# The last group's v beside and behind the last q and k, in a decoder layer on one core

## The reference, cut to what matters

```python
# B, S, D = 16, 128, 256; H, DH = 8, 64; f32 throughout
q, k, v = x @ W_q.T, x @ W_k.T, x @ W_v.T            # q, k: 512 wide, v: 256 wide
b = (q * k).reshape(B, S, H, DH).sum(-1) / sqrt(DH)
a = -softplus(x @ W_alpha_w.T + W_alpha_b).reshape(B, S, H, DH).sum(-1)
vs = where(sign(v) == 0, 1, sign(v)); vl = log(abs(v) + 1e-8)
# scan over time per batch and head, in logs: ln = lse(a_t + ln, b_t), nm likewise with b_t + vl_t,
#   y_t = sum over heads of sign * exp(nm - ln)
x = layernorm(x + y @ W_o.T)
x = layernorm(x + cross_attention_of_8_experts(x))    # relu(x @ in_e.T) @ out_e.T, gated
x = layernorm(x + three_layer_ffn(x))
```

## Time and profile before

| | us |
|---|---|
| median of 3 runs (lowest, highest) | 799.23 (799.13, 799.63) |
| the profiled execution's own time | 798.58 |
| its span, first to last instruction | 796.8 |
| mean granted clock, as a share of full speed | 0.998 |
| TensorE busy | 783.4 |
| VectorE, ScalarE, GpSimd busy | 473.9, 355.1, 199.8 |

### The profile page before, as it was taken

The page is one execution under the profiler, slowest core; times in us unless marked ns, Lnnn a source line. Parts: engine busy times, 40 slices in busy tenths (PEclk is TensorE's granted clock), DMA queues, the critical chain, the costliest instruction groups (busy, mean ns, idle before and its releaser), DMA issues.

```text
span 796.8 us, 12545 instructions
## 1 busy us (share of the span) xinstructions
PE 783.4 (98%) x3879; PEld 660.4 (83%) x3879; DVE 473.9 (59%) x1125; ACT 355.1 (45%) x683; POOL 199.8 (25%) x230
## 2 busy tenths in 40 slices
PE   8999989999999999999999999999999999999996
PEld 6888968888888888888888888888888888888885
DVE  4788878876686868778665664126422552255124
ACT  6788633444343434343443364434543354335331
POOL 3776143225352525344342310000000000000000
PEclk9999999999999999999999999999999999999999
DMA  9600000003113121311211000000000000000000
GB/s 335 207 1 0 2 1 1 1 1 107 56 52 107 49 85 53 105 53 55 92 41 53 4 5 1 1 0 27 0 0 0 26 0 0 0 19 9 1 0 30
DMA packets 15748, 31.45 MB, mean 39 GB/s; under 512 B 1616, under 2 KB 6224, under 8 KB 15440
## 3 DMA queue, kind: packets, MB, share of 16 engines
q1 hardware_dynamic: 15264, 30.04, 11.7%
q10 hardware_dynamic: 432, 0.79, 0.3%
HBM read 28.72 MB, written 2.10 MB: 39 GB/s over the span
## 4 chain that ended last, share of the span: by engine, by line
PE 93%; DVE 3%; issue 1%; DMA 1%; ACT 0%; POOL 0%; DVEq 0%; SPq 0%
PE bank L1046 29%; PE bank L961 14%; PE bank L838 9%; PE bank L866 8%; PE bank L939 7%; PE bank L940 7%; PE bank L944 7%; PE bank L960 6%; PE bank L1061 3%; PE bank L964 2%; DMA wp_lo_f<-in_wproj 1%; DVE x_tok L1184 1%; DVE hx_lo L1273 0%; PE bank L924 0%; PE bank L983 0%
## 5 line engine op out<-in xcount | busy, mean ns | idle before, releaser
L961 PE MATMUL bank<-wx_both,hx_hi 128*128 128x512 f32 x512 | 191.4, 397 | 0.0
L721 ACT ACTIVATE hx_hi<-bank 128x512 fp32r<-128x512 f32 x128 | 76.5, 598 | 205.3 <-PE bank L944 205.3
L537 POOL TENSOR_TENSOR x_tok<-right,x_tok 128x256 f32<-128x256 f32 x128 | 98.2, 768 | 212.2 <-ACT right L728 212.2
L1273 DVE SCALAR_TENSOR_TENSOR hx_lo<-bank,hx_hi 128x512 fp32r<-128x512 f32 x128 | 87.9, 687 | 66.6 <-ACT hx_hi L721 66.3
L961 PEld LDWEIGHTS bank<-wx_both,hx_hi 128*128 128x128 f32 x512 | 96.0, 188 | 16.7
L960 PE MATMUL bank<-wx_both,hx_lo 128*128 128x256 f32 x384 | 108.6, 283 | 0.0
L939 PE MATMUL bank<-xT_hi,wx_both 128*128 128x512 f32 x256 | 100.5, 392 | 0.9 <-ACT xT_hi L714 0.5
L1046 PE MATMUL bank<-ha_hi_r,wf_hi_r 128*128 128x512 f32 x256 | 100.0, 391 | 0.0
L1046 PE MATMUL bank<-hb_hi_r,wf_hi_r 128*128 128x512 f32 x256 | 99.9, 390 | 0.0
L940 PE MATMUL bank<-xT_hi,wx_both 128*128 128x512 f32 x256 | 99.7, 389 | 0.0
L1046 PE MATMUL bank<-ha_lo,wf_hi_r 128*128 128x512 f32 x256 | 99.6, 389 | 0.0
(11 more groups left out here) (157 smaller groups left out, 1443.2 us busy)
## 6 DMA issues: line engine op xcount, KB each, us to landing
stage<-in_wffn SPq DMA_DIRECT2D x44, 256.0 KB, 2.6
wx_raw<-in_wx SPq DMA_DIRECT2D x16, 512.0 KB, 3.7
x_tok<-in_x SPq DMA_DIRECT2D x1, 2048.0 KB, 12.2
out<-x_tok SPq DMA_DIRECT2D x16, 128.0 KB, 1.7
xs_lo_f<-in_xT SPq DMA_DIRECT2D x3, 512.0 KB, 5.8
wp_lo_f<-in_wproj SPq DMA_DIRECT2D x2, 512.0 KB, 7.7
ctx_sb<-in_ctx SPq DMA_DIRECT2D x1, 1024.0 KB, 7.9
itok_sb<-in_itok SPq DMA_DIRECT2D x1, 1024.0 KB, 9.9
```

The source lines that it names most:

```text
L537: pool.tensor_tensor(row, right[:, j % 2], row, ALU.add).then_inc(s_row_ok, 1)
L721: act.activation(hx_hi[:, place, c], bank[b][:, :], ACT.Relu).then_inc(s_relu_ok, 1)
L961: mm = pe.matmul(DBANK[j][:, :].rearrange("p (h d) -> p h d", h=2), hx_hi[:, place, c, a], wo_hl[:, :, c], start=(c == 0), stop=(c == XC - 1))
L1273: dve.scalar_tensor_tensor(out=hx_lo[:, place, c], in0=bank[b][:, :], scalar=0.0, in1=hx_hi[:, place, c].bitcast(F32), op0=ALU.max, op1=AL ...
```

## The change

TensorE no longer makes the last group's v behind t = 12. The first chunk stands between k of t = 14 and q of t = 15, the second behind k of t = 15. The transposes of a and b stand right behind it, ahead of all outputs, and the outputs fall into 6, 4 and 6 around the transpose of BT and the matmul of the extremes. The 16 unread matmuls are gone. `UBANK` is now banks 1, 2, 4, 5.

For the last group ScalarE makes v's sign in two instructions (`sign_v`: Sign of -v, then Sign of that minus 0.5), and VectorE adds it in one (`last_v`), the first chunk ahead of aT, the second between decT and the wait for the exponentials. q*k of t = 14 moves from GpSimd to VectorE, and ScalarE's copy of that k is gone. W_o's low half moves from VectorE to GpSimd, ahead of the two `low_v` of the last group. The reduction of v's sizes moves from the chain to a place behind the second `row_sum`. Two pieces of `expert_high(1, 1)` stand between ScalarE's signs, the other two behind `halves_x(0)`.

```diff
-        UBANK = [bank[i] for i in (6, 7, 1, 2)]
+        UBANK = [bank[i] for i in (1, 2, 4, 5)]
...
             groups_behind(pool, project)
+            pool.wait_ge(s_wo_hi_ok, 1)
+            pool.tensor_tensor(wo_lo[:, :, :], wo_raw[:, :, :], wo_hi[:, :, :].bitcast(F32), ALU.subtract).then_inc(s_wo_lo_ok, 1)
+            n = (G - 1) * DC
+            low_v(n, G - 1, 0)
+            low_v(n + 1, G - 1, 1)
...
+            def sign_v(c):
+                act.wait_ge(s_v_mm, n + c + 1)
+                act.wait_ge(s_v_out, n + 2)
+                if c > 0:
+                    act.wait_ge(s_vsign_ok, c)
+                act.activation(sgn[:, :], bank[6 + c][:, :], ACT.Sign, scale=-1.0).then_inc(s_vraw_ok, 1)
+                act.wait_ge(s_vraw_ok, c + 1)
+                act.wait_ge(s_vlo_ok, n + c + 1)
+                act.activation(vp[:, c], sgn[:, :], ACT.Sign, bias=neghalf[:, 0:1]).then_inc(s_vsign_ok, 1)
+
+            sign_v(0)
+            expert_high(1, 1, (0, 1))
+            sign_v(1)
+            high_v(n, G - 1, 0)
+            for t in range(2):
+                copy_u(t)
             act.wait_ge(s_tab_d, 2)
             act.activation(decT[:, :], decT[:, :], ACT.Exp).then_inc(s_tab_exp, 1)
             act.activation(betT[:, :], betT[:, :], ACT.Exp).then_inc(s_tab_exp, 1)
-            for t in range(2 * J, B):
...
-            expert_high(1, 1)
+            for t in range(2, 5):
+                copy_u(t)
+            high_v(n + 1, G - 1, 1)
+            for t in range(5, B):
+                copy_u(t)
...
             halves_x(0)
+            expert_high(1, 1, (2, 3))
...
-            for t, n in ((B - 2, 0), (B - 1, 0), (B - 2, 1), (B - 2, 2), (B - 1, 1), (B - 1, 2)):
+            for t, n in ((B - 2, 0), (B - 1, 0), (B - 2, 1), (B - 2, 2)):
                 project(t, n)
+            values(G - 1, (0,))
+            project(B - 1, 1)
+            project(B - 1, 2)
+            values(G - 1, (1,))
...
-            for _ in range(IDLE):
-                pe.matmul(bank[0][:, 0:P], ident[:, :], ident[:, :], start=True, stop=True)
...
+            def last_qk(t):
+                dve.wait_ge(s_q_out, t + 3)
+                dve.wait_ge(s_k_mm, t + 1)
+                dve.tensor_tensor(qk[:, t % 2], q_sb[:, t % 2], bank[t % 2 * 3 + 2][:, :], ALU.mult).then_inc(s_qk_ok, 1)
+                b_sum(t, t % 2)
+            last_qk(B - 2)
             a_sum(B - 1, 1)
...
+            last_qk(B - 1)
+
+            def last_v(c):
+                dve.wait_ge(s_vsign_ok, c + 1)
+                dve.scalar_tensor_tensor(out=vp[:, c], in0=vp[:, c], scalar=-EPS, in1=bank[6 + c][:, :],
+                                         op0=ALU.mult, op1=ALU.add).then_inc(s_v_out, 1)
+            last_v(0)
...
+            last_v(1)
             dve.wait_ge(s_tab_exp, 2)
```

More of the change, by code:

```diff
@@ L34 @@
 LOWEST = -3.0e38
-IDLE = 16
 WARM = 8
@@ L175, in decoder_kernel @@
         s_v_out = sem("v_out")
+        s_vraw_ok = sem("vraw_ok")
+        s_vsign_ok = sem("vsign_ok")
         s_u_mm = sem("u_mm")
@@ L510, in project @@
                         low_half(t + J)
-                    if j < J - 1 or not last:
+                    if j < J - 2 or not last:
                         pool.wait_ge(s_k_out, t + 3)
@@ L517, in project @@
                     at = j - (2 if first else 1)
[L518 to L521, removed]
+                    if 0 <= at < DC and not last:
                         low_v(g * DC + at, g, at)
@@ L660, in project @@
                     if j == J - 2 and last:
+                        logarithm(t, r)
                         absolute(t + 1, 1 - r)
@@ L664, in project @@
                     act.activation(q_sb[:, r], bank[r * 3 + 1][:, :], ACT.Copy).then_inc(s_q_out, 1)
-                    if j < J - 1 or not last:
+                    if j < J - 2 or not last:
                         logarithm(t, r)
+                        act.wait_ge(s_k_mm, t + 1)
+                        act.activation(k_sb[:, r], bank[r * 3 + 2][:, :], ACT.Copy).then_inc(s_k_out, 1)
                     if j == J - 2 and last:
@@ L669, in project @@
                         logarithm(t + 1, 1 - r)
-                    if j < J - 1 or not last:
-                        act.wait_ge(s_k_mm, t + 1)
-                        act.activation(k_sb[:, r], bank[r * 3 + 2][:, :], ACT.Copy).then_inc(s_k_out, 1)
                     if first:
@@ L698, in expert_high, with copy_u @@
                     act.activation(wx_hi[:, e, a], wx_raw[:, e, a], ACT.Copy).then_inc(s_wxhi_ok, 1)
-            for t in range(2 * J):
+            def copy_u(t):
                 act.wait_ge(s_u_mm, t + 1)
                 act.activation(u_sb[:, t], UBANK[t % 4][:, 0:D], ACT.Copy).then_inc(s_u_out, 1)
+            n = (G - 1) * DC
+            def sign_v(c):
[13 more added lines that the diff above has]
+                copy_u(t)
             act.wait_ge(s_tab_d, 2)
@@ L844, in three, with values @@
                 return [(a_hi, b_hi), (a_hi, b_lo), (a_lo, b_hi)]
-            def values(g):
+            def values(g, chunks=range(DC)):
                 pe.wait_ge(s_wp_lo_ok, 4 * DC)
                 pe.wait_ge(s_xs_lo_ok, g * J + J)
-                for o in range(DC):
+                for o in chunks:
                     pe.wait_ge(s_v_out, g * DC + o + 1)
@@ L879, in _ @@
                     project(t, n)
-                if t % J == (0 if t >= J else 1):
+                if t % J == (0 if t >= J else 1) and t < B - J:
                     values(t // J)
-            for t, n in ((B - 2, 0), (B - 1, 0), (B - 2, 1), (B - 2, 2), (B - 1, 1), (B - 1, 2)):
+            for t, n in ((B - 2, 0), (B - 1, 0), (B - 2, 1), (B - 2, 2)):
                 project(t, n)
+            values(G - 1, (0,))
+            project(B - 1, 1)
+            project(B - 1, 2)
+            values(G - 1, (1,))
             def output(t):
@@ L891, in output @@
                     vT_hi[:, c, a], vT_lo[:, c, a], wo_hi[:, c], wo_lo[:, c])], s_u_mm)
[L893 to L900, removed]
             pe.wait_ge(s_sp_ok, B + 2)
@@ L904, in _ @@
             pe.transpose(bank[3][:, 0:P], b_tok[:, :, :].rearrange("p b h -> p (b h)"), ident[:, :]).then_inc(s_ba_T, 1)
-            for t in range(2 * J - 1, 3 * J + 1):
+            pe.wait_ge(s_wo_lo_ok, 1)
+            pe.wait_ge(s_q_out, B + 2)
+            pe.wait_ge(s_qk_ok, B + 2)
+            for t in range(6):
                 output(t)
@@ L908, in _ @@
             pe.transpose(bank[0][:, P:2 * P], BT[:, :], ident[:, :]).then_inc(s_B_T, 1)
-            output(3 * J + 1)
+            for t in range(6, 10):
+                output(t)
             pe.wait_ge(s_extremes_ok, 1)
             pe.matmul(bank[3][0:1, P:P + 3], ones[:, :], extremes[:, :], start=True, stop=True).then_inc(s_extremes_T, 1)
-            for t in range(3 * J + 2, 4 * J):
+            for t in range(10, B):
                 output(t)
             pe.wait_ge(s_c_ok, 1)
-            for _ in range(IDLE):
-                pe.matmul(bank[0][:, 0:P], ident[:, :], ident[:, :], start=True, stop=True)
             pe.wait_ge(s_u_out, B + 4)
@@ L1134, in project @@
                         a_sum(t - 1, 1 - r)
+                        if j == J - 2 and last:
+                            dve.wait_ge(s_a_mm, t + 2)
+                            dve.tensor_tensor(al[:, 1 - r], bank[(1 - r) * 3][:, :], bias_b[:, :], ALU.add).then_inc(s_al_out, 1)
                         if j < J - 1 or not last:
                             b_sum(t - 1, 1 - r)
-                    if j == J - 2 and last:
-                        dve.wait_ge(s_a_mm, t + 2)
-                        dve.tensor_tensor(al[:, 1 - r], bank[(1 - r) * 3][:, :], bias_b[:, :], ALU.add).then_inc(s_al_out, 1)
                     if j == 1 and not first and not last:
@@ L1144, in project @@
                             gate((g - 1) * 2 + j // 2, e, masked[:, e])
-                    if j == 2 and last:
-                        dve.wait_ge(s_wo_hi_ok, 1)
-                        dve.tensor_tensor(wo_lo[:, :, :], wo_raw[:, :, :], wo_hi[:, :, :].bitcast(F32), ALU.subtract).then_inc(s_wo_lo_ok, 1)
                     at = j - (2 if first else 1)
[L1149 to L1152, removed]
+                    if 0 <= at < DC and not last:
                         take_v(g * DC + at, at)
@@ L1155, in _ @@
             groups_behind(dve, project)
-            a_sum(B - 1, 1)
[L1158 to L1163, removed]
+            def last_qk(t):
[4 more added lines that the diff above has]
+            last_qk(B - 2)
+            a_sum(B - 1, 1)
+            last_qk(B - 1)
[4 more added lines that the diff above has]
+            last_v(0)
             def group_row(g, j):
@@ L1229, in _ @@
             dve.tensor_scalar(extremes[:, 0:1], lowest[:, 1:2], RAISED, None, ALU.mult)
-            dve.tensor_reduce(extremes[:, 1:2], v_sizes[:, :], AX_X, ALU.max).then_inc(s_extremes_ok, 1)
             dve.wait_ge(s_B_T, 1)
@@ L1240, in _ @@
```

(3 more changed lines are left out.)

2 lines of the change are left out of this document (removed).

## The result

| | before | changed |
|---|---|---|
| median (lowest, highest) of 8 runs, us | 799.12 (798.39, 799.66) | 797.12 (795.65, 798.24) |
| the profiled execution, us | 798.58 | 797.46 |
| its span, us | 796.8 | 795.7 |

The ratio of the changed kernel to before is 0.9971, 95% interval 0.9962 to 0.9980: faster by 0.2 to 0.4%. The forecast was 797.0, in the likeliest of its cases. The total is right, but in part by luck: two of its terms are wrong, and they nearly cancel.

The account below looks back on a forecast made before the run. TensorE, busy 783.4 of 796.8 us, was taken as the bound. aT 4.55 us earlier, less two GpSimd holds of about 1.1 each, was taken as 2.2 gained: 799.23 - 2.2 = 797.0 us, range 795.3 to 798.4.

Parts of the forecast that it names:

- the likeliest of its cases: GpSimd's two `low_v` each hold a VectorE instruction of the chain: chance 0.48, own range 796.6 to 797.5 us.
- Projections and the start of the chain: Last group's projections to aT: q*k of t = 15 starts at 82.8, aT at 84.75 instead of 89.30, 4.55 us gained.
- Sign: ScalarE's sign instructions for the last v: 0.6 us each, bounds nothing and 1.2; rows above 0.7 would show it wrong.
- ScalarE's lateness of 0.45 us: Ahead of the exponentials: signs, expert pieces and copies keep ScalarE until 87.1, where the exponentials were due at 86.7.
- GpSimd beside the chain: During the tables and BT or AT: each `low_v` holds one VectorE instruction, costing about 1.1 us each time.
- the branch in which BT, not AT, is the one held: At the second `low_v`: BT transposed at 91.4, rows' transposes at 99.5, a gain of 1.9 us.
- TensorE behind BT: From BT to the rows' transposes: they start at 99.1 or 99.5 instead of 101.43, gaining 2.3 or 1.9 us.
- the clock falls: Rival: TensorE's wait for BT lowers the clock; up to 0.12 us more per output matmul, net +1.4, 800.6 us; chance 0.07.
- Should reach the end one to one: Behind 101.43 all is untouched and waits for TensorE, so the stretch's gain or loss reaches the end unchanged.
- The forecast of 2.2: Gain taken at the rows' transposes with both holds, between 2.3 us if AT is held and 1.9 if BT is.
- The unread matmuls: Behind TensorE's last output: 3.74 us off the path; without them TensorE waits 0.6 us instead of filling.
- The two expert pieces behind `halves_x(0)`: On ScalarE: 1.1 us inside its wait for the first product; without that cover, the first relu delayed by up to 1.1.

Follow-up runs that it names:

- the second profile of the changed kernel: The changed kernel run again with no edit, against before: 797.43 us median, ratio 0.9977; the profiled execution took 796.62 us.
- the five runs with 1.77: The changed kernel with only the first of GpSimd's two low halves waiting, for the second decT: 796.27 us, ratio 0.9968.

## Why the prediction was right, and where it wasn't

- **Projections and the start of the chain: right.** aT at 84.7 to 84.9 was forecast, 84.83 came; q*k of t = 15 started at 82.91 for 82.8. That the place itself fits so well is partly the start of this run, since aT spreads by 1 us; from q*k to aT it is 1.92 us for the 1.95 forecast. The "sixty" matmuls of t = 13 to 15 are 54 (12.24 us at 0.227); nothing was worked out from the count.
- **Sign: right in the main.** 0.57 from PSUM, 0.72 from SBUF with the bias tile, for 0.6 each. The second is above the 0.7 that was named as a sign of being wrong, and makes the pair 0.1 us longer than forecast. ScalarE's lateness of 0.45 us was right: 0.41 where nothing holds decT.
- **GpSimd beside the chain: right, and shown.** decT's second instruction 1.26 and BT 1.23, where both were forecast at above 1, in the branch in which BT, not AT, is the one held. TensorE's transpose of BT stands at 91.15; the branch had 91.4. Moving GpSimd's turn alone gave both back. The trace agrees with the Trainium skill's rule (SBUF — State Buffer, "SBUF: two separate sides") also in what it exempts: with the low halves late, `last_v`, whose second operand is in PSUM, took its usual 0.68 us across the start of GpSimd's instruction, and the scan behind it, with both in SBUF, waited.
- **TensorE behind BT: the size was off.** The text had 99.5 for the transposes in this branch. Where the clock stays that is what is measured: aT + 14.67 is 99.50. In 20 of 30 runs 1.5 us come on top. The rival "the clock falls" had a chance of 0.07 as a case that replaces the forecast; it is a term inside it, on two runs in three. Its mechanism and place were named rightly, its length was overrated: 16 matmuls, not 30, and 0.09 us each, not up to 0.12, and so it never decided the sign. "Clock 1.00 throughout" and L944 at 99 to 99.5 did not come true in the profile (0.91 and 0.67 in two stretches, 101.02).
- **"Should reach the end one to one": wrong.** This is the term that paid for the clock. From the first rows' transposes to those of the next group before had 14.23 us (101.43 to 115.66), the changed kernel 12.99, and 13.30 without the fall of the clock. In before, a sum of VectorE there was itself held by GpSimd's low halves of an expert (rows of GpSimd, VectorE and TensorE):
```profile
102.42 5.03 POOL L543 TENSOR_TENSOR wx_both<-wx_raw,wx_both 128x512 fp32r<-128x512 f32 x4
...
106.34 1.39 DVE L1184 SCALAR_TENSOR_TENSOR x_tok<-u_sb,c_tok,x_tok 128x256 f32<-128x256 f32 x1
...
115.66 0.33 PE L924 MATMUL bank<-ident,x_tok 128*128 128x128 f32 x1 [0.76 <-DVE x_tok L1262]
```
  and after it is not, and TensorE no longer waits at the second transposes:
```profile
103.27 2.54 POOL L546 TENSOR_TENSOR wx_both<-wx_raw,wx_both 128x512 fp32r<-128x512 f32 x2 [0.92 <-ACT wx_both L698]
...
105.74 0.48 DVE L1206 SCALAR_TENSOR_TENSOR x_tok<-u_sb,c_tok,x_tok 128x256 f32<-128x256 f32 x1
...
114.01 0.33 PE L944 MATMUL bank<-ident,x_tok 128*128 128x128 f32 x1
```
  TensorE comes later to the transposes than the rows are ready (98.37 and 101.02, for 100.96 and 101.43), so GpSimd, which goes by the rows, is further ahead of it: it ends 4.79 us behind TensorE's first transpose, for 6.02. The sum gives 0.91 of the 1.24 us. Another 0.34 lies in the transposes themselves: with all rows ready, the eight take 0.79 us from the first start to the last, for 1.13. Where the clock stays, as in the second profile of the changed kernel, the sum is still held for a part of its old time:
```profile
104.69 0.93 DVE L1206 SCALAR_TENSOR_TENSOR x_tok<-u_sb,c_tok,x_tok 128x256 f32<-128x256 f32 x1
```
  I had the row of before and left it out of the sum. No experiment was made for this hold, but the runs vary it. Over all profiles of the changed kernel and its variants the distance is 12.98 to 13.14 us where the sum took 0.48, 13.16 to 13.30 at 0.91 to 0.94, and 13.45 at 1.08 and 1.09. And before without its unread matmuls, whose sum took 0.48, had 0.9 of the 1.1 us that the clock cost it back.
- **The sum.** 0.4 us at the first transposes (2.3 or 1.9 forecast), 1.65 at the second (115.66 to 114.01), and 1.4 at VectorE's last row of the output (792.34 to 790.96); the whole span is 1.1 shorter. Without the fall of the clock it is 1.9 and 2.9 at the first two (84.83 + 14.67 = 99.50, and 13.30 more). The forecast of 2.2 lies between the two kinds of run, and the ratio of all is 2.3 us. That it is this near is luck: the fall of the clock (1.5 us in two runs of three) and the gain behind the transposes (0.9 to 1.2) were both at nothing in the forecast.
- **The unread matmuls** were called off the path. At the place where they stood that is right. Their use was the clock, and the change opened a wait of its own without one. The two expert pieces behind `halves_x(0)` cost nothing, as forecast: ScalarE still waited 0.71 us for the first product behind them.

## What to carry to other kernels

When a chain of small dependent VectorE instructions is on the critical path, look for what GpSimd does beside it, and give GpSimd its turn by a semaphore of that chain: two waits, which add no work, brought 2.6 us on the same chip (1.4 of them in the chain). Shortening one engine's work can open a wait in TensorE's midst; a filler belongs in the new wait, not where the old one was. And when a path is shortened, follow it past the first place where engines meet: here the next 14 us gave another 0.9 to 1.2 us, about as much as the clock took on average.

## What the runs showed of the hardware that was not expected

- A wait of TensorE of 2.04 us amid dense matmuls was followed by the lower clock level in one profile of the changed kernel and not in another; a third, with 2.03 us, has it again. By the mean clock it came in 20 of the 30 runs. Matmuls in the wait kept the full level (0.25 us of wait left). Waits of 0.66, 1.09 and 1.77 us were followed by the full level in the profiles taken, but two of the five runs with 1.77 have the lower mean clock; one of 2.80 us was followed by the full level in the one profile with it, and 8 of that kernel's 11 runs have the lower mean clock.
- Between two dependent VectorE instructions of 0.3 us there is room for GpSimd to take the port: its row starts at 86.20, during the first decT (86.14 to 86.42), and the second decT, from 86.47, ends 0.15 us behind it.
